# Scores and across-chunk outputs of a linear-attention layer: stationary operands of 64 rows by 128 columns for two of 64 by 64

## The chip, the cores and the metric

One core of a Trainium2 chip runs the whole program. The metric is the device time of one launch in microseconds (us), and lower is better. The time before is the median of three runs; the profile is of one further execution.

## What is computed

Eight sequences of 512 tokens with 128 features go through a transformer layer with linear attention (16 heads of 64) and a feed-forward part of 512, then a layer norm, then a mixture of 8 experts of which each token takes two, then a layer norm. The part that matters here is the attention:

```python
Q = _phi((x @ Wq).reshape(b, t, H, DH)).transpose(0, 2, 1, 3)     # phi = elu + 1
K = _phi((x @ Wk).reshape(b, t, H, DH)).transpose(0, 2, 1, 3)
V = (x @ Wv).reshape(b, t, H, DV).transpose(0, 2, 1, 3)
S = jnp.cumsum(jnp.einsum('bhti,bhtj->bhtij', K, V), axis=2)
z = jnp.cumsum(K, axis=2)
num = jnp.einsum('bhti,bhtij->bhtj', Q, S)
den = jnp.maximum(jnp.einsum('bhti,bhti->bht', Q, z), EPS_DEN)[..., None]
out = (num / den).transpose(0, 2, 1, 3).reshape(b, t, H * DV) @ Wo
```

The running sums are not formed token by token. A sequence is cut into 4 chunks of 128 tokens. Within a chunk, a token's output is the masked product of its scores (query times keys) with the values. From earlier chunks it is the query times a state, the sum of key times value over all chunks before. A column of ones beside the 64 values gives the denominator, so a state has 65 columns.

## The kernel before

The work is in two parts. The attention part runs over 8 sequences b and, in each, over 8 pairs of heads p; a step g = 8b + p handles one pair. The two heads of a pair lie in the two halves of the 128 partitions: `qT` and `kT` hold queries and keys with 64 features of head 0 in partitions 0 to 63 and of head 1 in 64 to 127, and 512 tokens along the free dimension. The feed-forward part, the gate and the routing of sequence b - 1 are spread over the steps of sequence b. The second part runs the experts over 39 tiles of 256 routed rows. Each engine has its own program, written out by hand; semaphores alone order them.

Every TensorE (PE) call of the attention on plain f32 operands shows in the trace as two weight loads and two matmuls. What PE does in step g, in this order (function, lines):

- `columns(g - 1)`, lines 514 and 521: the states' increments of 3 chunks, with stationary operands of 128 rows by 64 columns (6 calls), then the outputs inside the 4 chunks from the masked scores, 128 rows by 64 columns (16 calls). It waits at line 517 for the masked scores (`a_msk`).
- in p = 2 and p = 3 some transposes of other stages (`y_t`, `front_t`).
- `across(g - 1)`, lines 526 to 533: queries of chunks 1 to 3 as the stationary operand, the state as the moving one (65 columns). It waits for the state (`s_sb`, made by DVE at lines 1284 and 1286) and sends `o_mm`, on which DVE takes the denominator (L1270), the reciprocal (L1272) and the normalised output (L1274, `o_sb`).
- waits at lines 568 to 574: `q_phi` and `k_phi` (DVE, L1245, after four operations of ACT, L873 to L881), `v_sb`, `ot_lo` (DVE, L1117, the low half of the transposed output of the pair before), and in p = 4 `gelu_sb`.
- `scores(g)`, lines 535 to 542: keys of a chunk stationary, its queries moving (128 columns). It sends `sc_mm`, on which DVE masks (L1261, `a_msk`).
- `keys_t(g)`, a transpose of the keys; the projections of the next pair, `q_proj` and `k_proj`; `wo_acc`, the output projection of an earlier pair; `v_proj`, which waits for `a_msk`; `otr`, the transposes of the normalised output. In some p, work of sequence b - 1 follows.

DVE handles its work in the order: the state (L1284, L1286), `oT_lo` (L1117), den and normalisation, mask, work of other stages, q_phi, k_phi. The last across, `across(g_last)` at line 733, stands in the expert part between the first tiles' transposes.

Before the change each product of 128 rows of output (the tokens of a chunk) is made in two calls, one for each half of the stationary operand's columns, so that a stationary operand has 64 rows (the features of one head) and 64 columns (half a chunk). The loop in `scores`, with `HEADS` the two halves of partitions:

```python
for c in range(CH):
    for n, rows in enumerate(HEADS):
        for h, hs in enumerate(HEADS):
            mm = pe.matmul((bkE, bkF)[h][rows, blk(c)], kT[cur][hs, blk(2 * c + n, DH)],
                           qT[cur][hs, blk(c)], start=True, stop=True)
```

The output of half n goes to the partitions of half n; the two heads write to two banks of PSUM.

Of the kernel before, what the change touches and what calls it, by code (L numbers as in the profile page):

```python
# [32 lines left out]
CH = T // P  # L33
H, DH = 16, 64
PAIRS = H // 2
DV1 = DH + 1
# [26 lines left out]
def build(nc, x_d, ln1_g, ln1_b, wq_d, wk_d, wv_d, wo_d, ln2_g, ln2_b, wf1_d, wf2_d,  # L63
# [5 lines left out]
    with ExitStack() as ctx:  # L69
        def sb(name, shape, dt=F32):  # L70
            return ctx.enter_context(nc.sbuf_tensor(name, shape, dt))
# [35 lines left out]
        state = sb("state", [P, CH - 1, DV1])  # L107
# [5 lines left out]
        def take(n, back=None):  # L113
            if back is not None:
                spot[0] = back
            a = spot[0]
            spot[0] += n
            return work[:, a:a + n]
# [4 lines left out]
        qT = [take(T) for _ in range(2)]  # L123
        kT = [take(T) for _ in range(2)]
# [69 lines left out]
        start = sb("start", [P, 2 * E + 1])  # L194
# [34 lines left out]
        bkE, bkF = sc_banks[:, 0:512], sc_banks[:, 512:1024]  # L229
        bkG, bkH = o_banks[:, 0:512], o_banks[:, 512:1024]  # L230
# [179 lines left out]
        def _(pe):  # L410
# [6 lines left out]
            def blk(c, n=P):  # L417
                return slice(c * n, (c + 1) * n)
# [86 lines left out]
            HEADS = [slice(h * DH, (h + 1) * DH) for h in range(2)]  # L505
# [18 lines left out]
            def across(g):  # L524

                cur = g % 2
                pe.wait_ge(s_sb, g + 1)
                for c in range(1, CH):
                    for n, rows in enumerate(HEADS):
                        for h, hs in enumerate(HEADS):  # L530
                            mm = pe.matmul((bkG, bkH)[h][rows, blk(c, DV1)], qT[cur][hs, blk(2 * c + n, DH)],  # L531
                                           state[hs, c - 1, :], start=False, stop=(c == CH - 1))
                mm.then_inc(o_mm, 1)

            def scores(g):
                cur = g % 2
                for c in range(CH):
                    for n, rows in enumerate(HEADS):
                        for h, hs in enumerate(HEADS):
                            mm = pe.matmul((bkE, bkF)[h][rows, blk(c)], kT[cur][hs, blk(2 * c + n, DH)],  # L540
                                           qT[cur][hs, blk(c)], start=True, stop=True)
                mm.then_inc(sc_mm, 1)

            def keys_t(g):
# [8 lines left out]
            def step(b, p):  # L553
# [4 lines left out]
                if g > 0:  # L558
                    columns(g - 1)
                    if p == 2 and not first:  # L560
                        a_free(g - 1)
                        y_t(b - 1, bkA)
                    if p == 3 and not last:
                        b_free(g - 1)
                        front_t(b + 1)
                    across(g - 1)
# [6 lines left out]
                if p == 4 and not first:  # L573
                    pe.wait_ge(gelu_sb, b * NF)
                scores(g)
                if p != 3:
                    keys_t(g)
# [153 lines left out]
            pe.wait_ge(cnt_sb, B)  # L731
            rows_t(0)
            across(g_last)
            otr(g_last)
            rows_t(1)
# [1093 lines left out]
```

## Time and profile before

| | |
|---|---|
| median of 3 runs | 733.05 us (732.95 to 735.28) |
| the profiled execution | 734.17 us |
| its span | 732.4 us, 1.8 us less than its time |
| mean granted clock of TensorE | 0.98 of full speed |
| busy over the span: PE, its loads, DVE, ACT, POOL | 675.5, 576.5, 530.6, 436.1, 246.1 us |
| scores, 2048 loads and 2048 matmuls | 57.5 and 71.1 us busy |
| across, 1536 loads and 1536 matmuls | 28.4 and 37.3 us busy |

The attention part takes the span's first 541 us, some 65 us a sequence, the expert part the rest. PE is the row of matmuls, PEld that of the weight loads, which run beside them. Busy time of a row is the time in which at least one of its instructions is under way, so instructions that run side by side count once: a smaller busy sum of a line does not by itself make the program shorter. To read how fast instructions follow each other, one takes N of them from a row of the timeline, which gives the time from the first start to the last end, subtracts one instruction's own duration and divides by N - 1. What an engine's step costs the program is seen in what stands right behind it: either the engine starts the next thing at once, or it sits idle until another engine is ready.

### The profile page before, as it was taken

What the parts mean: (1) busy time and instruction counts of PE and PEld (TensorE: products, weight loads), DVE (VectorE), ACT (ScalarE), POOL (GpSimd) and SP (SyncE); (2) the same over time, 40 slices, a digit from 0 to 9 for tenths busy, and PEclk for the clock granted to TensorE, in tenths of its full rate; (3) what the DMA queues carried; (4) which work ended last, traced back from release to release, by engine and by line L of the source; (5) the groups of instructions that cost most, each with busy time, mean ns of one, the idle gap of its engine ahead of it and who ended that gap; (6) DMA issues with size and microseconds to landing.
All of it is one profiled execution on the core that took longest, in us unless ns stands there. A gap on an engine that the chain in (4) does not pass through costs nothing.

```text
span 732.4 us, 23390 instructions
## 1 busy us (share of the span) xinstructions
PE 675.5 (92%) x9372; PEld 576.5 (79%) x9372; DVE 530.6 (72%) x1552; ACT 436.1 (60%) x848; POOL 246.1 (34%) x288
## 2 busy tenths in 40 slices
PE   3798999999999999999999999999889996999983
PEld 2677888888888888888888888887669895999963
DVE  4767787887788788787878777777777684465681
ACT  5565576558447664846575675567336563566645
POOL 3000013025214302431340233124135567265775
PEclk9999999999999999999999999999999998899997
DMA  7600010001101000110110010001131123253625
GB/s 238 146 17 16 3 31 16 16 18 46 30 11 49 20 17 17 45 31 10 31 38 17 18 31 2 20 14 31 44 83 53 48 75 126 83 167 100 214 70 158
DMA packets 46522, 40.29 MB, mean 55 GB/s; under 512 B 9104, under 2 KB 41232, under 8 KB 46416
## 3 DMA queue, kind: packets, MB, share of 16 engines
q1 hardware_dynamic: 35360, 25.25, 12.3%
q0 software_dynamic: 4784, 10.39, 4.2%
q10 hardware_dynamic: 6272, 3.16, 1.5%
q8 instruction: 76, 1.25, 0.7%
q14 instruction: 30, 0.25, 0.1%
HBM read 23.12 MB, written 15.66 MB: 53 GB/s over the span
## 4 chain that ended last, share of the span: by engine, by line
PE 64%; DVE 16%; ACT 8%; issue 5%; DMA 2%; DVEq 1%; ACTq 1%; SPq 1%; POOL 0%; POOLq 0%
PE banks_sc L540 8%; PE banks_o L521 6%; PE bank_u L425 5%; PE banks_o L531 4%; PE banks_o L691 4%; PE bank_u L514 4%; PE bank_q L413 2%; PE bank_q L415 2%; PE bank_q L414 2%; DVE work L1245 2%; PE banks_sc L425 2%; PE bank_k L413 2%; PE bank_k L415 2%; PE bank_k L414 2%; PE bank_y L413 2%
## 5 line engine op out<-in xcount | busy, mean ns | idle before, releaser
L1684 POOL DMA_INDIRECT routed_rows<-routed,slot x64 | 62.9, 982 | 149.0 <-PE banks_sc L540 120.5
L811 ACT ACTIVATE work<-bank_u 128x512 f32<-128x512 f32 x64 | 38.3, 598 | 121.8 <-PE bank_u L425 121.8
L1261 DVE TENSOR_TENSOR work<-banks_sc,causal 128x1024 f32<-128x1024 f32 x64 | 77.9, 1218 | 3.2 <-PE banks_sc L540 2.1
L540 PE MATMUL banks_sc<-work 64*64 64x128 f32 x2048 | 71.1, 276 | 5.8 <-ACT v_aug L811 1.2
L691 PE MATMUL banks_o<-w,work 128*128 x624 | 75.7, 275 | 0.0
L1245 DVE SCALAR_TENSOR_TENSOR work<-bank_q,work 128x512 f32<-128x512 f32 x64 | 43.8, 684 | 42.5 <-ACT work L875 42.3
L691 PEld LDWEIGHTS banks_o<-w,work 128*128 128x128 f32 x624 | 72.7, 192 | 0.1
L521 PE MATMUL banks_o<-v_aug,work 128*64 128x65 f32 x2048 | 71.4, 223 | 0.0
L1652 POOL TENSOR_SCALAR ve<-mv 128x4 f32<-128x4 f32 x24 | 4.7, 194 | 194.5 <-DVE mv L1127 194.3
L540 PEld LDWEIGHTS banks_sc<-work 64*64 64x64 f32 x2048 | 57.5, 134 | 11.4 <-issue 9.7
L521 PEld LDWEIGHTS banks_o<-v_aug,work 128*64 128x64 f32 x2048 | 66.0, 139 | 0.0
L1245 DVE SCALAR_TENSOR_TENSOR work<-bank_k,work 128x512 f32<-128x512 f32 x64 | 44.2, 691 | 27.3 <-ACT work L881 27.3
L1762 POOL DMA_INDIRECT expert_results<-work x40 | 40.2, 1005 | 38.7 <-ACT work L993 29.0
L1674 POOL TENSOR_TENSOR gT_lo<-work,gT_hi 128x512 fp32r<-128x512 f32 x28 | 37.1, 1345 | 47.3 <-DVE gT_hi L1175 47.3
L425 PE MATMUL bank_u<-ident,work 128*128 128x128 f32 x284 | 46.6, 287 | 0.0
L1274 DVE TENSOR_TENSOR work<-banks_o,rden 128x512 f32<-128x512 f32 x64 | 44.3, 692 | 2.2
L531 PE MATMUL banks_o<-state,work 64*64 64x65 f32 x1536 | 37.3, 227 | 9.0 <-DVE state L1286 8.9
L1762 POOL DMA_INDIRECT expert_results<-work,xg_more x38 | 38.2, 1005 | 21.8 <-ACT work L993 13.6
L1117 DVE TENSOR_TENSOR oT_lo<-banks_sc,oT_hi 128x512 fp32r<-128x512 f32 x64 | 43.6, 681 | 1.3 <-ACT oT_hi L811 1.3
L873 ACT ACTIVATE work<-bank_q 128x512 f32<-128x512 f32 x64 | 38.3, 598 | 8.6 <-PE bank_q L415 4.6
L875 ACT ACTIVATE work<-work 128x512 f32<-128x512 f32 x64 | 40.4, 632 | 2.0
L881 ACT ACTIVATE work<-work 128x512 f32<-128x512 f32 x64 | 40.4, 631 | 2.0
(322 smaller groups left out, 1803.2 us busy)
## 6 DMA issues: line engine op xcount, KB each, us to landing
work<-in_L_attn_x SPq DMA_DIRECT2D x16, 256.0 KB, 3.6
work<-routed_rows SPq DMA_DIRECT2D x20, 132.0 KB, 2.1
xg_more<-routed_rows SPq DMA_DIRECT2D x19, 132.0 KB, 2.2
stage<-in_L_ffn_w SPq DMA_DIRECT2D x8, 256.0 KB, 2.7
moe_input<-routed SPq DMA_DIRECT2D x8, 256.0 KB, 2.2
work<-moe_input ACTq DMA_DIRECT2D x8, 256.0 KB
v_aug<-expert_results SPq DMA_DIRECT2D x4, 512.0 KB, 7.4
out<-work SPq DMA_DIRECT2D x6, 256.0 KB, 4.1
```

The source lines that it names most:

```text
L413: pe.matmul(out, w[0][:, wcols], m[0][:, mcols], start=first, stop=False)
L425: mm = pe.transpose(out[:, blk(c)], src(c), ident[:, :])
L521: pe.matmul((bkG, bkH)[h][rows, blk(c, DV1)], am[h][:, c, rows], va[:, c, 2 * p + h, :], start=(c == 0), stop=False)
L531: mm = pe.matmul((bkG, bkH)[h][rows, blk(c, DV1)], qT[cur][hs, blk(2 * c + n, DH)], state[hs, c - 1, :], start=False, stop=(c == CH - 1))
L540: mm = pe.matmul((bkE, bkF)[h][rows, blk(c)], kT[cur][hs, blk(2 * c + n, DH)], qT[cur][hs, blk(c)], start=True, stop=True)
L691: mm = pe.matmul(Y[t % 2][:, blk(k)], hTe[t % 2][:, f, blk(k)], w2[:, bass.ds(e[t] * F + f * D, D)], start=(f == 0), stop=(f == NF - 1))
L1117: return dve.tensor_tensor(out, whole, f32(high), ALU.subtract)
L1245: return dve.scalar_tensor_tensor(out=out, in0=pre[:, :], scalar=0.0, in1=e, op0=ALU.max, op1=ALU.add)
L1261: dve.tensor_tensor(am_all, sc_banks.rearrange("p (x s) -> p x s", s=P), causal[:, :].unsqueeze(1).broadcast_to([P, 2 * CH, P]), ALU.mult) ...
L1274: dve.tensor_tensor(on.rearrange("p c (h j) -> p h c j", h=2), o4[:, :, :, 0:DH], rden[:, :].rearrange("p (h c) -> p h c", h=2).unsqueeze( ...
L1684: pool.indirect_dma_start(rows_d, bass.IndirectOffsetOnAxis(slot[:, k, c:c + 1], 0), routed[:, c, k, :], None).then_inc(sct, 16)
L1762: pool.indirect_dma_start(res_d, bass.IndirectOffsetOnAxis(xg[n][:, k, D:D + 1].bitcast(U32), 0), yw[t % YRING][:, k, :], None).then_inc(r ...
```

## The change

The inner loop over the two halves of the stationary operand's columns goes away in `across` and in `scores`. A call takes all 128 columns (the tokens of a chunk) of one head's 64 rows, and writes all 128 partitions of the head's bank. Moving operands, banks, semaphores and waits stay as they were, as do `columns` and everything else.

```diff
                 pe.wait_ge(s_sb, g + 1)
                 for c in range(1, CH):
-                    for n, rows in enumerate(HEADS):
-                        for h, hs in enumerate(HEADS):
-                            mm = pe.matmul((bkG, bkH)[h][rows, blk(c, DV1)], qT[cur][hs, blk(2 * c + n, DH)],
-                                           state[hs, c - 1, :], start=False, stop=(c == CH - 1))
+                    for h, hs in enumerate(HEADS):
+                        mm = pe.matmul((bkG, bkH)[h][:, blk(c, DV1)], qT[cur][hs, blk(c)],
+                                       state[hs, c - 1, :], start=False, stop=(c == CH - 1))
                 mm.then_inc(o_mm, 1)
 
             def scores(g):
                 cur = g % 2
                 for c in range(CH):
-                    for n, rows in enumerate(HEADS):
-                        for h, hs in enumerate(HEADS):
-                            mm = pe.matmul((bkE, bkF)[h][rows, blk(c)], kT[cur][hs, blk(2 * c + n, DH)],
-                                           qT[cur][hs, blk(c)], start=True, stop=True)
+                    for h, hs in enumerate(HEADS):
+                        mm = pe.matmul((bkE, bkF)[h][:, blk(c)], kT[cur][hs, blk(c)],
+                                       qT[cur][hs, blk(c)], start=True, stop=True)
                 mm.then_inc(sc_mm, 1)
```

Nothing changes its place. On PE, a step's calls before, from `columns` to the first projection (the shape is that of the output, a count stands for calls in a row):

```order
L521 MATMUL banks_o<-v_aug,work 64x65 x16
L531 MATMUL banks_o<-state,work 64x65 x12
L540 MATMUL banks_sc<-work 64x128 x16
L425 MATMUL bank_u<-ident,work 128x128 x4
L413 MATMUL bank_q<-hT_hi,wq_hi 128x512
```

and the same place with the change (across is now line 530, scores line 538):

```order
L521 MATMUL banks_o<-v_aug,work 64x65 x16
L530 MATMUL banks_o<-state,work 128x65 x6
L538 MATMUL banks_sc<-work 128x128 x8
L425 MATMUL bank_u<-ident,work 128x128 x4
L413 MATMUL bank_q<-hT_hi,wq_hi 128x512
```

Across has 6 calls for 12 and scores 8 for 16, with outputs of 128 partitions for 64; their neighbours are the same. Over the program that is 64 times each.

## Rows read from the trace of the kernel before

**Rows 1.** The page, part 4: the chain that ended last, by engine, then by line
```profile
PE 64%; DVE 16%; ACT 8%; issue 5%; DMA 2%; DVEq 1%; ACTq 1%; SPq 1%; POOL 0%; POOLq 0%
PE banks_sc L540 8%; PE banks_o L521 6%; PE bank_u L425 5%; PE banks_o L531 4%; PE banks_o L691 4%; PE bank_u L514 4%; PE bank_q L413 2%; PE bank_q L415 2%; PE bank_q L414 2%; DVE work L1245 2%; PE banks_sc L425 2%; PE bank_k L413 2%; PE bank_k L415 2%; PE bank_k L414 2%; PE bank_y L413 2%
```

**Rows 2.** Windows: sequence 4 (us, busy us by engine, granted clock, DMA share, GB/s)
```profile
276.10:341.40 65.30, 64.38 (x1026) 53.57 (x1020) 52.06 (x154) 41.11 (x72) 18.76 (x20) 1.00 0.09 26
```

**Rows 3.** Timeline of sequence 4, p = 5: start, us, engine, line, what [idle before]
```profile
317.00 1.02 PEld L521 LDWEIGHTS banks_o<-v_aug,work 128*64 128x64 f32 x32
317.94 0.68 DVE L1117 TENSOR_TENSOR oT_lo<-banks_sc,oT_hi 128x512 fp32r<-128x512 f32 x1
318.10 0.44 PEld L531 LDWEIGHTS banks_o<-state,work 64*64 64x64 f32 x24
318.10 0.58 PE L531 MATMUL banks_o<-state,work 64*64 64x65 f32 x24
318.74 0.89 PEld L540 LDWEIGHTS banks_sc<-work 64*64 64x64 f32 x32 [0.20 <-issue]
318.77 1.10 PE L540 MATMUL banks_sc<-work 64*64 64x128 f32 x32
319.93 1.23 DVE L1261 TENSOR_TENSOR work<-banks_sc,causal 128x1024 f32<-128x1024 f32 x1
322.83 0.40 PE L437 MATMUL banks_sc<-wv_hi,hT_hi 128*128 128x512 f32 x1
```

**Rows 4.** Line 540 over the span: idle of its engine before it (us, times)
```profile
  issue: 9.7, 46
```

**Rows 5.** Timeline of sequence 4, p = 3, loads
```profile
298.32 0.44 PEld L531 LDWEIGHTS banks_o<-state,work 64*64 64x64 f32 x24 [0.17 <-issue]
298.67 0.86 PEld L540 LDWEIGHTS banks_sc<-work 64*64 64x64 f32 x32
```

**Rows 6.** Timeline of sequence 4, p = 4, loads
```profile
308.53 0.44 PEld L531 LDWEIGHTS banks_o<-state,work 64*64 64x64 f32 x24
308.98 0.89 PEld L540 LDWEIGHTS banks_sc<-work 64*64 64x64 f32 x32
```

**Rows 7.** Lines 531, 540 and 521: one instruction's ns, min/median/max
```profile
L531 PEld LDWEIGHTS banks_o<-state,work x192: 129/134/136, 276.2 to 334.3; 64*64 64x64 f32 x192
L531 PE MATMUL banks_o<-state,work x192: 216/218/268, 276.2 to 334.4; 64*64 64x65 f32 x192
L540 PE MATMUL banks_sc<-work x256: 268/269/321, 276.8 to 335.5; 64*64 64x128 f32 x128
L521 PEld LDWEIGHTS banks_o<-v_aug,work x2048: 135/138/231, 24.8 to 540.8; 128*64 128x64 f32 x187
```

**Rows 8.** The gate's loads, 8 columns streamed: timeline, and one load's ns
```profile
331.59 0.97 PEld L489 LDWEIGHTS bank_q<-gw,work 128*128 128x128 f32 x8
L489 PEld LDWEIGHTS bank_q<-gw,work x56: 186/192/193, 135.7 to 531.3; 128*128 128x128 f32 x56
```

**Rows 9.** The second expert layer: timeline of one tile, and one matmul's ns
```profile
603.35 1.87 PEld L691 LDWEIGHTS banks_o<-w,work 128*128 128x128 f32 x16
603.46 1.95 PE L691 MATMUL banks_o<-w,work 128*128 x16
L691 PE MATMUL banks_o<-w,work x124: 272/275/372, 579.8 to 609.2; 128*128 x124
```

**Rows 10.** Waits of PE in sequence 0 (us in total, times, longest)
```profile
PE banks_o L531 <- DVE state L1286: 5.0, 5, 2.3
```

**Rows 11.** Sequence 4: DVE's waits before q_phi, and its timeline in p = 7
```profile
DVE work L1245 <- ACT work L875: 4.4, 5, 1.4
339.56 0.68 DVE L1245 SCALAR_TENSOR_TENSOR work<-bank_k,work 128x512 f32<-128x512 f32 x1
340.60 0.23 DVE L1284 COPY state<-bank_u 128x65 f32<-128x65 f32 x1 [0.36 <-PE bank_u L514]
```

**Rows 12.** The transposes' loads, 128 by 128: one load's ns
```profile
L425 PEld LDWEIGHTS banks_sc<-ident,work x256: 137/141/143, 32.0 to 545.3; 128*128 128x128 f32 x128
```

## The prediction

> **What bounds the kernel now.** I read the page first, then the chain, then one step of the attention loop in order of time, and last the rows that price a load. Of the chain that ended last 64% is PE's, and the line of the scores leads it with 8% of the span [rows 1]. So a nanosecond more or less on PE counts, unless PE waits right behind it. In a middle sequence of 65.3 us the granted clock is 1.00, the full 2.4 GHz, and PE is busy for 64.38 us [rows 2].
>
> The step in [rows 3] (sequence 4, p = 5) shows the place of the change. Across (L531) issues its first load at 318.10, scores (L540) at 318.74. The loads of across are over in 0.44 us, then the loader sits idle for 0.20 us. What ends that is the oT_lo subtraction on DVE (L1117, 317.94 + 0.68 = 318.62), for which scores waits at line 572. It stands behind the state additions on DVE, so it does not hang on across at all: **across has a cover here**. Of the 64 steps, 46 have such a pause before scores, 9.7 us in all, 0.21 each [rows 4]. In step p = 3 there is none: 298.32 to 298.67, 0.35 us [rows 5], since the transposes of the next sequence stand ahead of across there and oT_lo is ready in time. In p = 4 it is 308.53 to 308.98, 0.45 us [rows 6], since scores waits for the last GELU (line 574).
>
> **How many run at once.** Every f32 matmul of the code is two loads and two matmuls in the trace: 12 calls of across are 24, 16 of scores are 32. N of them in T with an own duration d start (T - d)/(N - 1) apart. Across: (0.44 - 0.134)/23 = 13.3 ns per load of 64 columns [rows 3, 7]. The outputs inside a chunk (L521), whose 128 by 64 operands can lie only two side by side: (1.02 - 0.138)/31 = 28.5 ns [rows 3, 7]. The own durations are alike (134 and 138 ns) and so is a round: 24 loads in rounds of four take 0.306/5 = at most 0.061 us a round, 32 in rounds of two 0.882/15 = 0.059. So today all four quarters of the array work at once, the two column halves too, and whether 64 or 128 rows are loaded makes no difference. That is the point against a gain: one 64 by 128 instruction does the work of two that already ran side by side.
>
> **What 128 columns cost.** The gate (L489) loads 128 by 128 and streams only 8 columns, so its pace is the load's: (0.97 - 0.192)/7 = 0.111 us [rows 8]. The second expert layer (L691) loads 128 columns and streams 128: (1.87 - 0.192)/15 = 0.112 us for a load, (1.95 - 0.275)/15 = 0.112 for a matmul [rows 9]. A load of 128 columns takes twice one of 64, and it runs under the matmul before it.
>
> The Trainium skill, page "TensorE: Matmul & The Clock Gate", section on what overlaps in Part 3, says a load overlaps running matmuls only where their row groups differ. Rows 9 contradict it: all 128 rows on both sides, and load and matmul together take what a load alone takes. By the rule the change would be the third rival below; by the row it is the sum.
>
> **The sum.** Across: 24 loads in six rounds of four become 12 in six rounds of two, each round one load of 128 columns at 0.111, so scores can load 6 x 0.111 = 0.667 us after across does. Against today:
> - 46 steps with a pause, 0.64 us now: +0.02 each, **+0.9**. The work that hides the rest is oT_lo on DVE; without it each would pay 0.32.
> - 9 steps without one (p = 3 of sequences 1 to 6, and steps 1, 3 and 4 of sequence 0), 0.35 now: +0.32 each, **+2.9**.
> - 7 steps p = 4, 0.45 now: +0.21 each, **+1.5**.
> - The last across, behind the attention loop: +0.3, since PE then waits for its result through DVE. (The 64th stands in a stretch of sequence 7 at a lower clock, 0.66 now; I leave it at nothing.)
>
> Scores: eight rounds of four become eight of two. A matmul of 128 columns and a load of 128 both take 0.112. Now the last matmul starts 0.03 + (1.10 - 0.269) = 0.86 us after the first load [rows 3, 7]. After: one load of 0.111, then 7 rounds of 0.112, 0.895. That is +0.035, in the nine steps without a pause some 0.06, as their first load ran under across: **+2.5**. Nothing hides this; what is late next is keys_t, then the projections, ACT's four operations and the scores of the next step.
>
> Together +8.1. In sequence 0 PE waits 5.0 us for the state additions on DVE [rows 10], which splits weights then; part of its 1.3 us (3 x 0.32, 8 x 0.04) drowns there, and I take off half: **+7.5 us**.
>
> What waits for across: o_mm comes 0.3 us later, and den, the reciprocal, the normalisation and the mask (319.93 to 321.16 in [rows 3]) move with it. I cost that at nothing: the mask is needed by the values' projection at 322.83 [rows 3], and DVE idles before k_phi or the state copy later. The tightest step is p = 7, where k_phi starts without a pause but DVE then waits 0.36 us for PE: more than 0.3. DVE waits for ACT before q_phi in 5 of 8 steps of a sequence [rows 11]. If the cover failed in the other three, it would be 24 x 0.3 = 7 us more.
>
> Unknown ends: downwards, rounds of 0.107 us, which a quarter of the array shows in scores today (4 x (1.10 - 0.269)/31 [rows 3, 7]), leave the 46 steps at nothing and scores at 0.111 + 7 x 0.107 = 0.86, nothing either; with sequence 0 left out, +3. Upwards, the 7 us of the paragraph above. I take 0.111 and 0.112 because their rows are loads of 128 columns. The sum stands against the profiled execution: 734.17 + 7.5 = 741.7 us. The median of the runs is 1.1 lower, so 733.05 + 7.5 = **740.6 us**.
>
> **Rivals.**
> - *Loads get quick: faster.* The transposes also load 128 by 128 and have an own duration of 141 ns [rows 12], like the 64-column ones. If a 64 by 128 load takes 0.06, across stays at 0.35, and scores need 0.06 + 7 x 0.107 = 0.81 in place of 0.86 (a quarter's matmuls in scores now start 4 x 26.8 ns apart, by [rows 3, 7]): 64 x -0.05 = -3.2, **729.9 us**. It decides where a load takes under some 0.07. Against it: plain f32 loads of 128 columns show 192 ns and 0.111 apart; the transposes are another kind of instruction.
> - *The waits take it all: no change.* Rounds of 0.107, and the 0.3 of p = 3 and p = 4 lost in waits further on (PE waits in p = 3 for k_phi before the feed-forward): about +2, **735 us**. Against it: k_phi hangs on projections that stand behind these very scores, so the wait moves along.
> - *No load under a matmul of the same rows.* A matmul of 63 columns more lasts 51 ns more [rows 7]: 0.81 ns a column, 0.053 us for 65, 0.104 for 128. Rounds become 0.111 + 0.053 and 0.111 + 0.104 if a load waits for the matmul on its rows to end: scores +0.76 in 64 steps, across +0.34, +0.63 and +0.53 in 46, 9 and 7: +74, **807 us**.
> - *The two row halves take turns.* 12 and 16 instructions one by one: scores +0.93, across +0.69, +0.98 and +0.88: +107, **840 us**. Against it: today rounds of four hold both halves.
>
> That the change does not do what it says is out: the calls are written by hand, and the program lists 6 and 8 calls of 128 columns of output for 12 and 16.
>
> **How the numbers follow.** A measurement of this kernel tells 0.3%, 2.2 us, from no change. Forecast 0.75, loads quick 0.06, waits take it all 0.08, no load under a matmul 0.05, turns 0.06. Faster 0.06, same 0.08, slower 0.86. The range runs from 735 (the case in which the waits take it all; the sum's own lower end is 736) to 748 (the sum and the 7 us of a failed cover, 747.6). It leaves out the quick loads and the two large losses, 0.17.
>
> **What the profile after would show.** Right: 12 loads for 24 in across and 16 for 32 in scores; across's loads spread over about 0.75 us with an own duration near 190 ns; its first load to that of scores 0.67 in nearly every step, the pause gone; scores' matmuls in about 1.1 us as before, with half as many; busy sums of both lines about halved and the span longer all the same. Wrong: loads of 64 by 128 that start 0.03 us apart (quick loads), or 0.11 apart (turns); a pause before scores that still stands; new idle time on DVE or PE behind the mask.

## The result, and the profile after

The changed kernel takes 743.64 us, the median of 4 runs (743.18 to 744.48), against 733.61 us (732.95 to 735.28, 4 runs) before. The ratio is 1.0129 with a 95% interval of 1.0109 to 1.0148. That is slower by 1.3%, inside the range and 3.0 us above the forecast of 740.6. The profiled execution took 744.06 us with a span of 742.3, 9.9 more than before.

From the page of the changed kernel, parts 1, 4 and 5. The columns of part 5 are busy us and mean ns of one, then the idle time before them and who ended it:

```profile
span 742.3 us, 19806 instructions
PE 689.9 (93%) x7580; PEld 599.1 (81%) x7580; DVE 529.3 (71%) x1552; ACT 436.6 (59%) x848; POOL 246.3 (33%) x288
PE 72%; DVE 11%; ACT 7%; issue 4%; DMA 2%; DVEq 1%; ACTq 1%; SPq 1%; POOL 0%; POOLq 0%
L538 PE MATMUL banks_sc<-work 64*128 64x128 f32 x1024 | 73.0, 282 | 1.5 <-ACT v_aug L809 1.5
L538 PEld LDWEIGHTS banks_sc<-work 64*128 64x128 f32 x1024 | 64.0, 190 | 1.9 <-ACT v_aug L809 1.9
L530 PE MATMUL banks_o<-state,work 64*128 64x65 f32 x768 | 57.0, 281 | 9.1 <-DVE state L1284 8.9
L530 PEld LDWEIGHTS banks_o<-state,work 64*128 64x128 f32 x768 | 48.1, 188 | 16.5 <-DVE state L1284 12.5
```

The two lines have half as many instructions, and PE is busy for 14.4 us more: 689.9 against 675.5. PE's share of the chain that ended last went from 64% to 72%, and DVE's fell from 16% to 11%. The busy sums did not fall as I had said they would. Scores went from 71.1 to 73.0 us, across even from 37.3 to 57.0. I had thought of the sum over instructions; a busy sum counts the time in which at least one runs, and that follows the time from the first start to the last end.

The same step as in [rows 3] (sequence 4, p = 5), timeline of the changed kernel. Across is now L530, scores L538, and every later line of the file has moved up by two:

```profile
324.57 0.68 DVE L1115 TENSOR_TENSOR oT_lo<-banks_sc,oT_hi 128x512 fp32r<-128x512 f32 x1
324.72 0.75 PEld L530 LDWEIGHTS banks_o<-state,work 64*128 64x128 f32 x12
...
325.39 0.98 PEld L538 LDWEIGHTS banks_sc<-work 64*128 64x128 f32 x16
325.44 1.12 PE L538 MATMUL banks_sc<-work 64*128 64x128 f32 x16
325.66 0.17 DVE L1268 TENSOR_SCALAR den<-banks_o 128x8 f32<-128x8 f32 x1 [0.41 <-PE banks_o L530]
326.70 1.21 DVE L1259 TENSOR_TENSOR work<-banks_sc,causal 128x1024 f32<-128x1024 f32 x1
329.51 0.40 PE L437 MATMUL banks_sc<-wv_hi,hT_hi 128*128 128x512 f32 x1
```

From across's first load to that of scores it is now 0.67 us, for 0.64. The pause is gone: oT_lo is over at 325.25, and scores starts only at 325.39, when the loads of across are through. So what was a wait for DVE has become PE's own time. The 12 loads take 0.75 us: five rounds of 0.111 to the start of the sixth, and the own duration of 0.188, are 0.743. Everything behind has the distances of before: the values' projection stands 4.79 us behind across, for 4.73.

Where there was no pause, in p = 3, and where there was a short one, in p = 4 (timeline of sequence 4, loads), the answers to [rows 5, 6] are

```profile
304.30 0.75 PEld L530 LDWEIGHTS banks_o<-state,work 64*128 64x128 f32 x12 [0.17 <-issue]
304.97 0.98 PEld L538 LDWEIGHTS banks_sc<-work 64*128 64x128 f32 x16
...
314.90 0.75 PEld L530 LDWEIGHTS banks_o<-state,work 64*128 64x128 f32 x12
315.56 0.98 PEld L538 LDWEIGHTS banks_sc<-work 64*128 64x128 f32 x16
```

0.67 and 0.66, for 0.35 and 0.45. By the starts of the single instructions it is 0.664 us in every step at full clock, whatever the step.

Sequence 4 by windows, the answer to [rows 2] (columns as there):

```profile
282.60:348.80 66.20, 65.95 (x802) 56.20 (x798) 51.76 (x154) 41.16 (x72) 18.77 (x20) 1.00 0.08 26
```

From the first scores of this sequence to the first of the next it is 66.19 us, for 65.26: +0.93 at the same clock of 1.00. **Over sequences 1 to 6 it is +0.91 in the mean, from 0.86 to 0.94.** Step by step, taken from the first load of scores to the next step's (us, sequence 1):

| from p to p + 1 | 0 | 1 | 2 | 3 | 4 | 5 | 6 | 7 |
|---|---|---|---|---|---|---|---|---|
| before | 6.958 | 7.650 | 7.247 | 10.309 | 9.765 | 7.641 | 8.279 | 7.416 |
| after | 7.019 | 7.700 | 7.620 | 10.582 | 9.823 | 7.682 | 8.351 | 7.400 |
| difference | +.061 | +.050 | +.373 | +.273 | +.058 | +.041 | +.072 | -.016 |

The forecast's terms give +0.06 for an ordinary step, +0.36 for the one that ends at p = 3 and +0.27 for the one that ends at p = 4. Only the step from p = 7 is off: it should have cost 0.06 and cost nothing. There PE waits for q_phi ahead of line 496, and DVE gets to q_phi no later than before, 4.28 us behind the first load of scores for 4.31. So PE waits 0.07 us less (sequence 4, before and after, loads):

```profile
339.69 0.10 PEld L496 LDWEIGHTS bank_q<-chosen,before 128*128 128x128 bf16 x1 [0.33 <-DVE work L1245]
346.43 0.10 PEld L496 LDWEIGHTS bank_q<-chosen,before 128*128 128x128 bf16 x1 [0.26 <-DVE work L1243]
```

What is left is sequence 0. It takes 3.0 us more (from 20.87 to 84.08, for 20.77 to 80.95), of which the rounds explain 1.4. The rest is here, in windows of the changed kernel:

```profile
60.00:62.00 2.00, 1.72 (x25) 1.72 (x27) 1.54 (x5) 0.00 (x0) 1.01 (x1) 0.86 0.23 86
62.00:64.00 2.00, 2.00 (x13) 1.68 (x11) 1.57 (x2) 0.24 (x1) 0.00 (x0) 0.50 0.00 0
64.00:66.00 2.00, 2.00 (x9) 1.58 (x8) 0.00 (x0) 1.30 (x3) 0.00 (x0) 0.79 0.00 0
```

and in a window of the kernel before:

```profile
62.00:64.00 2.00, 2.00 (x10) 1.54 (x10) 0.68 (x1) 1.80 (x3) 0.00 (x0) 1.00 0.00 0
```

After a wait of PE of 1.75 us for the state, the granted clock stands at 0.50, the 1.2 GHz level, for some three microseconds, and the step takes 8.83 us in place of 7.21. Before, PE waits there just as long, 1.75 us, and the clock stays at 1.00.

### The profile page after: what moved, and what is told of

Same layout as the page of the kernel before. It is cut to its first block, busy times and chain, and to the rows that moved or that the text cites. A ratio compares the mean times of both kernels' runs of the same rounds, so it can differ in the third digit from the quotient of the medians.

```text
span 742.3 us, 19806 instructions
## 1 busy us (share of the span) xinstructions
PE 689.9 (93%) x7580; PEld 599.1 (81%) x7580; DVE 529.3 (71%) x1552; ACT 436.6 (59%) x848; POOL 246.3 (33%) x288
## 4 chain that ended last, share of the span: by engine, by line
PE 72%; DVE 11%; ACT 7%; issue 4%; DMA 2%; DVEq 1%; ACTq 1%; SPq 1%; POOL 0%; POOLq 0%
PE banks_sc L538 8%; PE banks_o L530 7%; PE banks_o L521 6%; PE bank_u L425 5%; PE banks_o L689 4%; PE bank_u L514 3%; PE bank_q L413 3%; PE bank_q L415 3%; PE bank_q L414 3%; PE banks_sc L425 3%; PE bank_k L413 2%; PE bank_k L415 2%; PE bank_k L414 2%; PE bank_y L413 2%; PE bank_y L414 2%
## 5 line engine op out<-in xcount | busy, mean ns | idle before, releaser
L538 PE MATMUL banks_sc<-work 64*128 64x128 f32 x1024 | 73.0, 282 | 1.5 <-ACT v_aug L809 1.5
L538 PEld LDWEIGHTS banks_sc<-work 64*128 64x128 f32 x1024 | 64.0, 190 | 1.9 <-ACT v_aug L809 1.9
L530 PE MATMUL banks_o<-state,work 64*128 64x65 f32 x768 | 57.0, 281 | 9.1 <-DVE state L1284 8.9
L530 PEld LDWEIGHTS banks_o<-state,work 64*128 64x128 f32 x768 | 48.1, 188 | 16.5 <-DVE state L1284 12.5
L873 ACT ACTIVATE work<-work 128x512 f32<-128x512 f32 x64 | 40.5, 632 | 2.0
```

Of the source, the lines that this page charges most:

```text
L530: mm = pe.matmul((bkG, bkH)[h][:, blk(c, DV1)], qT[cur][hs, blk(c)], state[hs, c - 1, :], start=False, stop=(c == CH - 1))
L538: mm = pe.matmul((bkE, bkF)[h][:, blk(c)], kT[cur][hs, blk(c)], qT[cur][hs, blk(c)], start=True, stop=True)
```

## The experiments

All were compared with the kernel before on the chip on which they ran. The first four ran on one on which the kernel before takes 735.35 us. Which chip gave the result above is not known; by its time it is one like that, and both are called the first chip here. On the chips of the others, the second and the third, the kernel before takes about 769 us; what that does to the comparison is told with the runs that look at it.

### Scores alone, and across alone

Theory: what decides is rounds of loads, so the parts add up. Rival: something else than the load count sets the price. The first kernel has only the new `scores`, the second only the new `across`.

```diff
# scores_wide: across as before
-                    for n, rows in enumerate(HEADS):
-                        for h, hs in enumerate(HEADS):
-                            mm = pe.matmul((bkE, bkF)[h][rows, blk(c)], kT[cur][hs, blk(2 * c + n, DH)],
-                                           qT[cur][hs, blk(c)], start=True, stop=True)
+                    for h, hs in enumerate(HEADS):
+                        mm = pe.matmul((bkE, bkF)[h][:, blk(c)], kT[cur][hs, blk(c)],
+                                       qT[cur][hs, blk(c)], start=True, stop=True)
```

> Only scores has stationary operands of 64 rows by 128 columns; across is as before. My theory (each part costs what its rounds cost, and the parts add up): scores from its first load to its last matmul goes from 0.866 to about 0.90 us, +0.035 in 55 steps and +0.06 in 9, so +2.5 us; the pause before scores stays in 46 steps. Rival 1, the extra 2 us over the sum come from scores (for instance from DVE or ACT getting their bank later): +4 us or more. Rival 2, fewer instructions help scores: below 0.

```diff
# across_wide: scores as before
-                    for n, rows in enumerate(HEADS):
-                        for h, hs in enumerate(HEADS):
-                            mm = pe.matmul((bkG, bkH)[h][rows, blk(c, DV1)], qT[cur][hs, blk(2 * c + n, DH)],
-                                           state[hs, c - 1, :], start=False, stop=(c == CH - 1))
+                    for h, hs in enumerate(HEADS):
+                        mm = pe.matmul((bkG, bkH)[h][:, blk(c, DV1)], qT[cur][hs, blk(c)],
+                                       state[hs, c - 1, :], start=False, stop=(c == CH - 1))
```

> Only across has the wide operands. My theory: its first load to that of scores is 0.664 us in every step in place of 0.643 (46 steps), 0.347 (9) and 0.45 (7): +0.9 + 2.9 + 1.5 + 0.3 = +5.6 us, and no idle time of the loader before scores. If the 1.6 us that the changed kernel lost in sequence 0 at the lower clock hang on the wide across, they come here too: +7.2 us. Rival, the wide across costs 0.3 us in every step: +19 us.

Scores alone: 741.61 us against 735.35, ratio 1.0085 (1.0057 to 1.0112). Across alone: 749.97, ratio 1.0200 (1.0175 to 1.0224). Both miss upwards, and **across alone is slower than the whole change**. Sequence 4 takes 65.87 us with scores alone (+0.61), 66.77 with across alone (+1.51), and 66.19 with both (+0.93): the parts sum to 2.12, over twice the whole. The timelines say why. Across alone, p = 5 and then p = 3 of sequence 4:

```profile
328.35 0.75 PEld L530 LDWEIGHTS banks_o<-state,work 64*128 64x128 f32 x12
329.16 0.86 PEld L539 LDWEIGHTS banks_sc<-work 64*64 64x64 f32 x32
...
307.75 0.75 PEld L530 LDWEIGHTS banks_o<-state,work 64*128 64x128 f32 x12 [0.17 <-issue]
308.57 0.86 PEld L539 LDWEIGHTS banks_sc<-work 64*64 64x64 f32 x32
```

Scores alone, p = 3 and then p = 5:

```profile
303.48 0.44 PEld L531 LDWEIGHTS banks_o<-state,work 64*64 64x64 f32 x24 [0.17 <-issue]
303.99 0.97 PEld L539 LDWEIGHTS banks_sc<-work 64*128 64x128 f32 x16
...
323.57 0.44 PEld L531 LDWEIGHTS banks_o<-state,work 64*64 64x64 f32 x24
324.21 1.00 PEld L539 LDWEIGHTS banks_sc<-work 64*128 64x128 f32 x16 [0.20 <-issue]
```

With across wide, scores starts 0.82 us behind it where with both wide it is 0.664, in every step: 0.15 more. With scores wide, p = 3 has 0.51 where the kernel before has 0.35: 0.16 more; in p = 5 it is 0.64 as before, since the pause hides it. So where the instructions change from tiles of 64 by 128 to tiles of 64 by 64 or back, PE pays 0.15 to 0.16 us once. Before, there is no such change between across and scores, and after, there is none either; each half of the edit alone puts one there. Across alone pays it 64 times (64 x 0.151 = 9.7 us), scores alone in p = 3 in full and in p = 4 in part (0.51 for 0.45). That accounts for a middle sequence. From across's first load to the transposes behind scores it is 0.815 + 1.034 = 1.849 us with across alone and 0.664 + 1.101 = 1.765 with both: 8 x 0.084 = 0.67 more, against 1.51 - 0.93 = 0.58 measured. For scores alone it is 0.16 + 0.06, and 8 x 0.055 for scores itself, 0.66 against 0.61 measured. The rest is in sequence 0, where the clock stands at 0.50 for 6.8 us in a row in both profiles: of the 7.1 us that the span with scores alone is longer, 3.4 lie in sequence 0, and of the 13.9 with across alone, 4.7.

The Trainium skill, page "TensorEngine Tiling (Array Packing)", section Key Properties, says that changing the tiling mode drains the TensorE. These runs agree that the change of mode costs something, 0.15 to 0.16 us for these two. How far the array empties they do not show: with across alone the first load of scores starts 0.815 us after that of across, ahead of the end at 0.887 that the trace models for the last matmul of across.

### Is it the loads that pace across?

In the changed kernel a call of across streams 8 of the 65 state columns. If matmuls had a part in the 0.111 of a round, across would shorten.

```diff
-                        mm = pe.matmul((bkG, bkH)[h][:, blk(c, DV1)], qT[cur][hs, blk(c)],
-                                       state[hs, c - 1, :], start=False, stop=(c == CH - 1))
+                        mm = pe.matmul((bkG, bkH)[h][:, c * DV1:c * DV1 + 8], qT[cur][hs, blk(c)],
+                                       state[hs, c - 1, 0:8], start=False, stop=(c == CH - 1))
```

> The changed kernel, but the matmuls of across stream 8 columns of the state in place of 65, so the rest of the state's columns are left out of the output. The loads are the same. My theory, a round of the wide across is one load of 128 columns: across keeps its pace (0.111 us a round, 0.664 to the first load of scores) and the time stays that of the changed kernel, +10 us against before, within 1. Rival, the matmuls also count (load and stream one after the other, or the stream alone): 57 columns at 0.81 ns are 0.046 us a round, 0.28 us per across, so up to 16 us less than the changed kernel.

744.83 us, ratio 1.0126 (1.0098 to 1.0154), where the change itself has 1.0129. Timeline, p = 5 of sequence 4:

```profile
325.34 0.75 PEld L530 LDWEIGHTS banks_o<-state,work 64*128 64x128 f32 x12
325.35 0.84 PE L530 MATMUL banks_o<-state,work 64*128 64x8 f32 x12
...
326.01 0.98 PEld L538 LDWEIGHTS banks_sc<-work 64*128 64x128 f32 x16
```

0.67 us from across to scores, with an eighth of the columns. The distance is 0.664 or 0.665 in every step of the middle sequences, and each of these sequences as a whole is within 0.02 us of the changed kernel's. The loads pace across, the matmuls lie fully under them. With that the rule of the third rival is out by a second way: a load that waited for its rows' matmul would have gained here.

### Do the two heads' rows work at once?

The loops of scores are exchanged, so that one head's four chunks come first and then the other's. Neighbouring instructions then have the same rows.

```diff
-                for c in range(CH):
-                    for h, hs in enumerate(HEADS):
+                for h, hs in enumerate(HEADS):
+                    for c in range(CH):
                         mm = pe.matmul((bkE, bkF)[h][:, blk(c)], kT[cur][hs, blk(c)],
                                        qT[cur][hs, blk(c)], start=True, stop=True)
```

> The changed kernel, but scores does the four chunks of head 0 first and then those of head 1, so that neighbouring instructions use the same 64 rows. My theory, the wide form lives on two row halves working side by side: now one instruction in 0.112 us, 0.111 + 15 x 0.112 = 1.79 us to the last matmul in place of 0.90, +0.89 in 64 steps, +57 us over the changed kernel, +67 against before. Rival, the order does not matter since PE looks ahead over more instructions: +10 us against before.

776.61 us, ratio 1.0574 (1.0541 to 1.0607): 41 us more than the kernel before, 33 more than the changed one. That lies between the two expectations. Timeline, scores of one step:

```profile
192.18 1.52 PEld L538 LDWEIGHTS banks_sc<-work 64*128 64x128 f32 x16
192.23 1.66 PE L538 MATMUL banks_sc<-work 64*128 64x128 f32 x16
```

1.52 us for 0.98, so +0.54 a step and not the +0.89 of sixteen turns one by one. By the single starts, five loads follow each other at 0.112, then come three pairs at that distance (the first at 0.558 and 0.560 us), then five single ones. The records do not name the head. With eight loads a head, I read it so that the first three of head 1 run beside the last three of head 0. PE then starts work on the free rows some three instructions early, not eight. So the two row halves do work at once in the changed kernel (the fourth rival is out), and it is the alternation of the heads in the code that feeds them. 64 x 0.54 = 35 us is about what the run lost.

### Where the cover is, and where not

Extra calls in across: 8 of 64 by 64 in the kernel before (0.23 us of loads by its own pace), 2 of 64 by 128 in the changed one (0.22). What they write goes to columns that nobody reads.

```diff
# extra_before, ahead of the calls of the last chunk
+                    if c == CH - 1:
+                        for x in (1, 2):
+                            for n, rows in enumerate(HEADS):
+                                for h, hs in enumerate(HEADS):
+                                    pe.matmul((bkG, bkH)[h][rows, blk(4, DV1)], qT[cur][hs, blk(2 * x + n, DH)],
+                                              state[hs, x - 1, :], start=False, stop=False)
```

> The kernel before with 8 more calls in across (16 instructions of each kind, four rounds of four, about 0.23 us), whose output goes to columns of the banks that nobody reads. My theory, the wait of scores for oT_lo covers across in 46 steps with a pause of 0.28 us: those pay nothing, the 9 steps without a pause 0.23, the 7 steps p = 4 about 0.13, the last across 0.23: +3.2 us. Rival, there is no cover (the pause only follows across): 64 x 0.23 = +14.7 us.

```diff
# extra_after, at the same place
+                    if c == CH - 1:
+                        for h, hs in enumerate(HEADS):
+                            pe.matmul((bkG, bkH)[h][:, blk(4, DV1)], qT[cur][hs, blk(1)],
+                                      state[hs, 0, :], start=False, stop=False)
```

> The changed kernel with 2 more calls in across (4 instructions of each kind, two rounds of two, 0.22 us), again into columns that nobody reads. My theory, the cover is used up there: all 64 steps pay, +14 us over the changed kernel, +24 against before. Rival, some cover is left: clearly less, down to +3 over the changed kernel.

The first takes 774.0 us against 769.26, ratio 1.0072 (1.0049 to 1.0096), so +4.7 us for 64 times 0.23 = 14.7. Its p = 0 of sequence 2:

```profile
146.81 0.32 PEld L537 LDWEIGHTS banks_o<-state,work 64*64 64x64 f32 x16
147.03 0.33 PEld L533 LDWEIGHTS banks_o<-state,work 64*64 64x64 f32 x16
147.27 0.21 PEld L537 LDWEIGHTS banks_o<-state,work 64*64 64x64 f32 x8
147.45 0.89 PEld L546 LDWEIGHTS banks_sc<-work 64*64 64x64 f32 x32
```

0.64 us from across to scores, as without the extra calls: they went into the pause. In sequence 1, against the profile of the kernel before on the first chip, the step to p = 3 pays 0.237, that from p = 3 to 4 0.158, that from p = 0 to 1 0.10, and the other five are within 0.03 of nothing. Some of the 4.7 us is no price of the calls in the pause: on this chip PE stops in the scores of p = 3 (more on that below), and from the first load of scores to the transposes it takes 2.92 to 2.95 us there in sequences 2 to 6, where `early_before`, a kernel with the old number of calls on the same chip, takes 2.44 to 2.68. The second takes 782.39 us; the changed kernel took 768.88 on the same chip, so +13.5 for 64 times 0.22 = 14.2, and in sequence 1 every step is 0.19 to 0.22 longer. So the pause is a cover in the kernel before, and in the changed kernel no cover is left.

### The cover taken away

In the kernel before, oT_lo ends the pause (L1117), and DVE does it behind the state additions. In p = 5 of sequences 1 to 6 it is ready to be done ahead of them.

```diff
+                ahead = p == 5 and 0 < b < B - 1
+                if ahead:
+                    ot_low(g - 2)
                 if g > 0:
                     states(g - 1)
-                if g > 1 and p != 4:
+                if g > 1 and p != 4 and not ahead:
                     ot_low(g - 2)
```

> The kernel before with oT_lo ahead of the state copies on DVE in the six steps p = 5 of sequences 1 to 6, where DVE idles 0.84 us before the state copy. My theory, oT_lo is what scores waits for: the pause before scores is gone in these six steps, 6 x 0.28 = -1.7 us. Rival, scores waits for something else there (q_phi, k_phi, or its own issue): the pause stays, 0 us.

766.26 us, ratio 0.9967 (0.9952 to 0.9982). Timeline, p = 5 of sequence 4:

```profile
321.85 0.69 DVE L1117 TENSOR_TENSOR oT_lo<-banks_sc,oT_hi 128x512 fp32r<-128x512 f32 x1
...
322.85 0.48 DVE L1286 TENSOR_TENSOR state<-bank_u,state 128x65 f32<-128x65 f32 x2
...
323.40 0.44 PEld L531 LDWEIGHTS banks_o<-state,work 64*64 64x64 f32 x24
...
323.75 0.87 PEld L540 LDWEIGHTS banks_sc<-work 64*64 64x64 f32 x32
...
324.05 0.17 DVE L1270 TENSOR_SCALAR den<-banks_o 128x8 f32<-128x8 f32 x1 [0.72 <-PE banks_o L531]
```

The pause is gone from this step, 0.35 us for 0.64, and the step from p = 4 to 5 falls from 9.765 us (the kernel before, first chip) to 9.471. Six such steps are 1.8 us, and the interval holds that. So the old form can go down to 0.35 there, where the new one shows 0.664 everywhere. The same edit on the changed kernel should then bring nothing:

> The changed kernel with the same reordering. My theory, scores starts right behind across there and has no pause left to win: the time stays that of the changed kernel, within 0.3 us by the trace, and the first load of across to that of scores stays 0.664. Rival, oT_lo still holds up scores in the changed kernel: -1.7 us.

767.29 us, ratio 0.9980 (0.9965 to 0.9995) against the old kernel on that chip, and the changed kernel itself 768.57. The steps that the edit touches, from p = 4 to 5 in sequences 1 to 6, take 9.80 to 9.82 us in both, and across to scores stays 0.664: in the trace the edit brings nothing. The median is 1.3 us lower all the same, more than the 0.3 allowed. The two profiled executions differ elsewhere: in sequence 0 by 1.5 us (one stretch at half clock for two), in sequence 7 by 1.6 the other way (one for none), and in the expert part by 2.6. None of that was shown to come from the edit. The old kernel with the edit was run once more there:

> The kernel before with oT_lo ahead of the state copies in six steps, as in early_before. By the trace of early_before each of the six steps is 0.29 us shorter: -1.8 us on any chip. If the -3 us measured there was the chip's own, less is left here.

767.95 us, ratio 0.9980 (0.9965 to 0.9995). So it is faster than the kernel before in both runs, by 0.3% and by 0.2%. Whether it beats the changed kernel on these chips is less clear: 766.26 us against 768.88 on the second, but 767.95 against 768.57 on the third, where single executions of either scatter over 5 to 7 us. On the first chip, where the old form is ahead by 10 us, the edit was not run. Only p = 5 was tried: of the 46 pauses six were taken away, and the others are untried.

### The same two kernels on other chips

Since the runs above were compared with the kernel before at 769 us and not 733, both kernels were run there as they are.

> The changed kernel once more, unchanged. If the stretch of about 3.3 us at half the clock in sequence 0 is a matter of chance, its profile need not show it, and its times should scatter between +8.5 and +10 us. If it hangs on where in time the wait before it falls, it is there again: +10 us, and the span is 742.3 within 0.5.

> The kernel before, unchanged, for its profile on the chip of this call. If this chip is like that of the run called after_again, where both kernels take about 769 us, the steps p = 3 of sequences 2 to 6 take about 11.7 us here in place of 10.3 and the expert part 220 us in place of 199, with PE and DVE stopped in the middle of scores; the time is 769 us. If it is like the first, they take 10.3 us and 199 us and the time is 733 to 735 us.

> The changed kernel, unchanged. On a chip like the first: +8 to +10 us against before. My theory says +8.3 by the rounds of across and scores (0.93 us a sequence) and the rest by stretches of half the clock in sequence 0, which come and go. On a chip like that of after_again: within 2 us of before, because the steps p = 3 stall there for 1.4 us with the old form and 0.4 with the new one.

The changed kernel: 768.88 us, ratio 0.9995 (0.9974 to 1.0017) on the second chip, and 768.57, ratio 0.9997 (0.9982 to 1.0011) on the third. The kernel before, run against itself on the third: 769.98, 1.0014 (0.9992 to 1.0036). **On those two chips the change makes no difference that could be measured**, and both kernels take some 25 to 36 us more than on the first. The two expectations that have a case for such a chip came true, but for the expert part (226.8 us for the 220 expected). The one that knew only the first chip did not, and its profile has two stretches at half clock in sequence 0, not one or none.

Sequence 1 is the same as on the first chip to within 0.03 us for both kernels, so the effect of the change is still there: 65.25 against 66.20. From sequence 2 on another loss takes it back. In p = 3, the step in which scores follows across without a pause, the kernel before shows this on the third chip (sequence 4, profile of the kernel before):

```profile
300.96 0.44 PEld L531 LDWEIGHTS banks_o<-state,work 64*64 64x64 f32 x24 [0.17 <-issue]
301.31 0.64 PEld L540 LDWEIGHTS banks_sc<-work 64*64 64x64 f32 x22
302.30 0.21 PEld L540 LDWEIGHTS banks_sc<-work 64*64 64x64 f32 x4 [0.35 <-issue]
303.03 0.23 PEld L540 LDWEIGHTS banks_sc<-work 64*64 64x64 f32 x6 [0.52 <-issue]
303.09 0.17 DVE L1270 TENSOR_SCALAR den<-banks_o 128x8 f32<-128x8 f32 x1 [1.05 <-remote]
```

and the changed kernel on the same chip this:

```profile
306.43 0.75 PEld L530 LDWEIGHTS banks_o<-state,work 64*128 64x128 f32 x12 [0.17 <-issue]
307.09 0.97 PEld L538 LDWEIGHTS banks_sc<-work 64*128 64x128 f32 x16
```

PE stops twice amid the scores, waiting for nothing that the profile shows, and at the same time DVE stands still for 1.05 us with den, though across had been over for a while. The changed kernel goes through its scores there without a stop, and loses some 0.4 us only at the projections behind them. The step from p = 3 to 4 takes 11.75 us before and 10.99 after, where on the first chip it was 10.31 and 10.59. Between the third chip's two profiles, before to after, the differences are: sequence 0 +4.6 (with two stretches at half clock after and none before), sequence 1 +0.95, sequences 2 to 6 -1.0, sequence 7 -1.4, the expert part -4.2, and the start +0.4, together -0.6, as the spans of 768.7 and 768.1 have it. So the stops in p = 3 take back some 5.6 us of what the change costs (5 times the +0.91 that is due, and the -1.0 that is there). The -1.4 of sequence 7 goes with a stretch at half clock that only the kernel before has there, and the -4.2 is from one execution of each: the changed kernel itself has 219.6 us in the expert part on the second chip and 222.5 on the third.

What the stops are is open; no run was made for them, but the traces narrow it down. They are in p = 3 of sequences 2 to 7 and not of sequence 1, and from sequence 2 on POOL scatters routed rows (L1684) in this step, the first time just as across starts. The scatter alone is not enough: it also stands in p = 0, 1 and 2, without a stop, and on the first chip at the same place in p = 3, without one. Across and scores have 112 loads and matmuls in the kernel before and 56 in the changed one. In `extra_before`, with 144, the stops are about 0.45 us longer; but the changed kernel loses 0.35 to 0.42 us in this step, and `extra_after`, with 64, only 0.09 to 0.14. So more instructions do not always go with a longer stop. In the expert part the clock has a share: behind the last scores it stands at 0.50 for 22 us of the kernel before on the first chip and for 49 on the third. Half speed for 27 us more is at most 13.5 of the 27.9 us by which this part is longer.

## Why the prediction was right

Point by point, in the terms of the profiled execution, 9.9 us measured and 7.5 forecast:

| | forecast | measured |
|---|---|---|
| sequence 0 and the start | +0.65 (half of 1.3) | +3.1 |
| sequences 1 to 6 | +5.7 (6 x 0.955) | +5.5 |
| sequence 7 | +0.6 | +0.8 |
| behind the attention loop | +0.3 | +0.5 |

The forecast column adds up to 7.3; the rest of the 7.5 is rounding in the sum.

- *A round of loads at 0.111 us, 0.667 from across to scores.* Right: 0.664 in every step, with 0.188 us own duration. The gate and the second expert layer, loads of 128 by 128, had the price of loads of 64 by 128. `short_stream` shows that it is the loads which set it.
- *The pause as cover.* Right: +0.04 to +0.07 in steps that had it, +0.37 and +0.27 where it was missing or short. `extra_before` filled it up with other work at nearly no cost, `extra_after` found none, and `early_before` turned it into time.
- *Scores +0.035, and 0.06 where there was no pause.* Right, with some scatter: in sequences 1 to 6 it is 1.097 to 1.106 us from the first load of scores to the transposes behind them in six of the eight steps, for 1.063 where there was a wait before scores (+0.04) and 1.037 in p = 3 (+0.06). In p = 2 and 6 it is 1.115 to 1.119, +0.05.
- *The shift of den, normalisation and mask costs nothing.* Right. DVE's waits are where that shows, by the waits of the changed kernel (us in all, times, longest):

```profile
DVE den L1268 <- PE banks_o L530: 14.6, 30, 1.6
```

  Before, it was 3.8 us in 5 waits. It waits longer before den, since across ends later, and no step of a middle sequence shows a cost beyond its rounds. The 7 us that I kept for a failed cover did not come. Step p = 7, the tightest by my reading, even gave 0.07 us back, as PE waits for DVE's q_phi there. It is the one step of a middle sequence where a wait behind took up the cost of the rounds, and it is not in the sum.
- *Half of sequence 0's 1.3 us drowns in PE's waits.* Wrong, and this is the term of the sum that I had mis-sized. PE waits there as long as before, 5.0 us in 5 waits in both [rows 10]; none of it drowned. My reading is that the longer PE work stands ahead of DVE's additions too and moves them along. The rounds make +1.4 us in sequence 0, where the whole by my terms is 1.3 and I had taken off half.
- *The clock.* Not foreseen: 1.6 us of the profiled execution's sequence 0 are a stretch at half clock, after a wait which the kernel before has too. It is no fixed price of the change. In sequence 0 the profiles of the old form show none (before, `before_again`, `extra_before`) or one stretch of 3.4 us (`early_before`, `early_again`); of the new form `heads_apart` shows none, the change, `early_after` and `short_stream` one, `after_again`, `after_third` and `extra_after` two; the two half edits show one of double length. Where there is one, its step is 1.1 to 1.6 us longer. The new form has more of them in these few executions; whether it causes them by where its waits fall was not shown.
- *Edits cost their sum.* The expectations for the two parts alone rested on that, and it failed; the prediction for the whole did not need it, because the whole has no change of tile form between across and scores.
- *The rivals.* Quick loads, loads that wait for the matmul of their rows, row halves in turns: each would show in the distance of loads, and 0.664 in every step excludes them. "The waits take it all" has no support on the first chip, where a middle sequence is longer by 0.91 us at the forecast 0.955.

The verdict itself holds for the first chip. On two others the ratio is 1, and the same forecast would have missed: the old form loses more there, in part by stops in p = 3 that are in no trace of the first chip. That the result was taken on a chip without them is luck.

## What to carry to other kernels

When small matmuls already share the array, count rounds and price a round by its longest part. Here twice the columns per load was half the calls and no gain, and a loss in across, where a stream of 65 columns is too short to cover the longer load (0.111 us a round for 0.061). Before costing the longer part in full, look at what PE does right behind it: where it stands idle for another engine the cost is hidden, and that idle time may itself be taken out by a reorder on the other engine, as in p = 5 here. And do not add up halves of an edit that change the form of tiles: measure the whole. A result of 1% on one chip is worth a second chip.

## What the runs showed that I had not expected

- Between tiles of 64 by 64 and of 64 by 128, in either order, PE starts 0.15 to 0.16 us later than between tiles of one form; under a pause that is hidden.
- With instructions of one head in a row, PE, as I read the starts, still begins the other head's some three instructions early, so one by one is not what exchanged loops give: 1.52 us for 16 loads, where 16 turns at 0.112 would be 1.87.
- A matmul of 8 columns on a 64 by 128 tile takes the same place in time as one of 65: the row of 12 has 0.84 us for 0.89.
- The granted clock stood at 0.50 for 3.4 us after a wait of PE of 1.75 us, and in another execution of nearly the same work not at all.
- The same kernel takes 733 us on one chip and 769 on two others. In sequence 1 they agree; the difference lies in p = 3 from sequence 2 on (10.31 us or 11.75), and in the expert part (198.9 us or 226.8 from the last scores to the end). Its cause stays open, and so does whether a form with fewer instructions is the better choice there.
